# A transformer layer and a graph layer in one kernel: eight buffers for the projection's input, finer waits into the feed forward, graph tiles begun between the shared products

## The chip, the cores and the metric

One Trainium2 chip, one core of it. The metric is the device time of one execution in microseconds (us), as the median of several executions.

## The reference

`x` is 2 x 2048 x 512 in float32 (4096 rows), `cond` one vector of 512 per batch. Cut to what is computed:

```python
# layer 0: conditioned transformer block
h = ada_ln(x, cond, Wln1, bln1)                 # layer norm, scale and shift from cond @ W + b
x = x + attn(h, Wq, bq, Wk, bk, Wv, bv, Wo, bo) # 16 heads of 32, softmax over 2048 keys, @ Wo + bo
h = ada_ln(x, cond, Wln2, bln2)
x = x + gelu(h @ W1 + b1) @ W2 + b2             # 512 -> 2048 -> 512
# layer 1: graph attention over the first NG = 20 rows of each batch, two directions d
q_exp = where(x.sum(-1) == 0, 0, cond)
sf = concat([x, q_exp]) @ W_self.T + b_self
out = sf
for d in (0, 1):
    kv = sf[:, :20]                             # scores of each row against 20 rows, 16 heads
    aff = (sf @ Wq[d].T + bq[d]) . (kv @ Wk[d].T + bk[d]) / sqrt(32), masked by adj, + bias
    out = out + (softmax(aff) @ kv) @ Wout[d] + bout[d]
return x + relu(out)
```

## The kernel before, in words

The program is written out by hand: each engine has its own list of instructions in a fixed order, and engines meet only through semaphores. A function `pe_...`, `act_...`, `dve_...`, `pool_...` or `sp_...` issues work for TensorE, ScalarE, VectorE, GpSimd or SyncE (which issues nearly all DMAs and, as the others, waits in order). A semaphore's count is what is waited for: `s_om` counts projection tiles that TensorE has finished, and so on. Products of float32 matrices are made from a high part (rounded to the matmul's type) and a low part (what the rounding left): `TRI` lists the three pairs high*high, high*low, low*high, so a product over 512 takes 3 x 4 = 12 matmuls of 128x128 by 128x512.

The stages are: q, k, v with the first layer norm; attention (32 units `v` of four heads by 512 queries); the output projection; the feed forward (8 chunks of 512 rows, 16 blocks `q` each, 128 in all); the graph's shared products; the graph's 32 row tiles. The change touches three places.

**The output projection** (`sp_out`, `pe_out`, `act_out`, `dve_out`, `pool_out`, lines 1008 to 1101) runs over 32 tiles `t` of 128 rows. For one tile: SyncE loads the attention output from memory into `ao` (three buffers, L960) and the residual rows into `x2` (five buffers, L967, two tiles ahead, once the store of five tiles earlier has landed); ScalarE copies `ao` into the high part of `aT` (L1057, two buffers, two tiles ahead); VectorE subtracts for the low part (L1070); TensorE does the 12 matmuls (L1045) into one of three banks of PSUM; GpSimd adds the bias to the residual (L1101); VectorE adds PSUM and residual (L1077); SyncE stores it to `x2_d` (L1021). In VectorE's order tile t is added first and then tile t+2 is split. Beside this run, at fixed tiles, the last unit's reciprocals (tile 2), the load of the feed forward's first chunk `xinb` (1 MB, L1005, tile 6), its layer norm (VectorE at tiles 8 to 11, GpSimd at tile 10), its transposes (four on TensorE before tiles 16 to 19), and the splitting of eight blocks of feed-forward weights (tiles 20 to 27; five of them are loaded at tiles 20 to 24, each once VectorE has split an earlier one).

The first two tiles are split during the last attention unit, and `pe_out_tile(0)` stands before that unit's last two value products (L729).

**The way into the feed forward.** `out_over` (L1103) waits for everything of the projection, the landing of the last stores of `x2` with it. All five engines call it first in the feed forward; ScalarE then also waits for `b2B`, the second bias (`s_bias` at 96), which SyncE loads after its own `out_over` and after four weight blocks (L1471 to 1473). A block q of the feed forward is `pe_ff1(q)` (L1181, 12 matmuls into bank 4 or 5), gelu on ScalarE (L1292), its split on VectorE (L1303, L1305) and `pe_ff2(q)` (L1194, 12 matmuls into banks 0 to 3). TensorE's order is ff1(0), ff1(1), ff2(0), ff1(2), ff2(1), and so on. ScalarE splits two weight blocks after each of the first 12 gelus (L470).

**The graph's start.** `pe_graph_shared` (L1571) makes products that all tiles share: `pe_ww`, `pe_gg` (L1547, split into `gg` by ScalarE L1600 and VectorE L1626), `pe_vw(0)`, `pe_vw(1)` (L1558, 16 matmuls each, masked into `vw` by VectorE L1633), and `pe_rows(0..3)` (L1567, 4 small matmuls each). Each of the four results of `pe_rows` goes through one buffer `rt`: ScalarE L1267, then VectorE L1312, L1314, L1317, one after the other. Only then do the tiles begin: `turn_x(0)` (transposes L1709, split by ScalarE L1801 and VectorE L1849), ScalarE's row sum (`act_zero`, L1795), VectorE's test of it (`dve_zero`, L1844), its transpose on TensorE (`turn_nz`, L1716), VectorE's edge terms (L1858 to 1867), the same for tile 1, and then score(0) (L1728, 24 matmuls, and L1734).

## Time and profile before

| | us |
|---|---|
| median of 3 executions | 3128.03 |
| lowest, highest | 3121.56, 3131.3 |
| the profiled execution, whole | 3132.72 |
| its span, first to last instruction | 3131.3 |
| TensorE busy in the span | 3076.8 (98%) |
| VectorE busy | 2156.5 (69%) |
| GpSimd busy | 1542.9 (49%) |
| ScalarE busy | 1388.4 (44%) |

Times in the views count from the span's start. "PE" is TensorE's matmuls, "PEld" its weight loads, "DVE" VectorE, "ACT" ScalarE, "POOL" GpSimd, "SPq" the queue in which SyncE issues DMAs. In brackets behind a piece of the timeline stands how long the engine was idle before it, and who ended that. PEclk is the share of the full clock that TensorE was granted.

### The profile page before, as it was taken

What the parts mean: (1) busy time and instruction counts of PE and PEld (TensorE: products, weight loads), DVE (VectorE), ACT (ScalarE), POOL (GpSimd) and SP (SyncE); (2) the same over time, 40 slices, a digit from 0 to 9 for tenths busy, and PEclk for the clock granted to TensorE, in tenths of its full rate; (3) what the DMA queues carried; (4) which work ended last, traced back from release to release, by engine and by line L of the source; (5) the groups of instructions that cost most, each with busy time, mean ns of one, the idle gap of its engine ahead of it and who ended that gap; (6) DMA issues with size and microseconds to landing.
All of it is one profiled execution on the core that took longest, in us unless ns stands there. A gap on an engine that the chain in (4) does not pass through costs nothing.

```text
span 3131.3 us, 42990 instructions
## 1 busy us (share of the span) xinstructions
PE 3076.8 (98%) x16138; PEld 2144.6 (68%) x16138; DVE 2156.5 (69%) x3633; ACT 1388.4 (44%) x2703; POOL 1542.9 (49%) x655
## 2 busy tenths in 40 slices
PE   8999999999999999999999999899999999999999
PEld 7887655555555555555555546688888888778998
DVE  4457889998999999989999976443333333237776
ACT  2221466666666666666666672221111111013333
POOL 0000389889888898898898973200000000102222
PEclk9999999999999999999999999999999999899999
DMA  6674687879779788797887776520111110212221
GB/s 206 187 228 150 175 169 169 193 150 198 167 165 201 151 189 174 167 199 150 181 182 160 164 155 230 187 81 6 35 41 41 41 41 29 98 59 68 78 82 61
DMA packets 169366, 423.39 MB, mean 135 GB/s; under 512 B 18493, under 2 KB 60605, under 8 KB 141864
## 3 DMA queue, kind: packets, MB, share of 16 engines
q0 software_dynamic: 27744, 201.08, 31.7%
q1 hardware_dynamic: 139639, 214.07, 22.8%
q10 hardware_dynamic: 1776, 5.51, 0.7%
q8 instruction: 128, 2.10, 0.3%
q14 instruction: 79, 0.64, 0.1%
HBM read 143.51 MB, written 75.50 MB: 70 GB/s over the span
## 4 chain that ended last, share of the span: by engine, by line
PE 94%; DVE 2%; DMA 2%; issue 1%; POOL 1%; ACT 1%; SPq 0%; DVEq 0%; ACTq 0%; POOLq 0%
PE ps L384 16%; PE ps L672 15%; PE ps L683 15%; PE ps L1194 12%; PE ps L1181 11%; PE ps L460 5%; PE ps L1728 4%; PE ps L464 3%; PE ps L1745 3%; PE ps L689 2%; PE ps L1766 1%; PE ps L1045 1%; PE ps L1531 1%; PE ps L158 1%; PE ps L293 1%
## 5 line engine op out<-in xcount | busy, mean ns | idle before, releaser
L397 DVE TENSOR_REDUCE nmp<-ps 128x1 f32<-128x512 f32 x1966 | 1200.0, 681 | 108.2 <-PE ps L384 103.9
L762 ACT ACTIVATE pt<-ps 128x512 f32<-128x512 f32 x2048 | 1031.0, 625 | 458.7 <-PE ps L672 455.5
L861 POOL TENSOR_TENSOR pt<-pt 128x2048 f32<-128x2048 f32 x217 | 995.9, 4589 | 119.6 <-ACT pt L762 113.3
L672 PE MATMUL ps<-qs,ks 128*128 128x512 f32 x2048 | 810.6, 400 | 2.5 <-ACT pt L762 2.5
L384 PE MATMUL ps<-ks,qs 96*128 96x512 f32 x1966 | 803.5, 409 | 0.1
L384 PEld LDWEIGHTS ps<-ks,qs 96*128 96x128 f32 x1966 | 372.6, 190 | 265.3 <-DVE nmp L397 167.8
L683 PE MATMUL ps<-pt,vq 128*32 128x512 f32 x4096 | 493.6, 599 | 0.0
L672 PEld LDWEIGHTS ps<-qs,ks 128*128 128x128 f32 x2048 | 389.4, 191 | 96.2 <-ACT pt L762 19.5
L1181 PE MATMUL ps<-hpb,w 128*128 128x512 f32 x1536 | 382.6, 399 | 3.4 <-DMA x_d<-x 3.4
L1194 PE MATMUL ps<-w,gp 128*128 128x512 f32 x1536 | 380.5, 396 | 3.1 <-DVE gp L1305 3.1
L1303 DVE CAST gp<-g 128x512 fp32r<-128x512 f32 x128 | 61.7, 482 | 403.7 <-ACT g L1292 403.7
L1194 PEld LDWEIGHTS ps<-w,gp 128*128 128x128 f32 x1536 | 289.4, 188 | 72.4 <-DVE gp L1305 3.5
L1181 PEld LDWEIGHTS ps<-hpb,w 128*128 128x128 f32 x1536 | 289.9, 191 | 70.2 <-issue 5.6
L1292 ACT ACTIVATE g<-ps,b1c 128x512 f32<-128x512 f32 x128 | 88.2, 689 | 535.9 <-PE ps L1181 535.9
L1425 POOL TENSOR_TENSOR res<-res,b2B 128x512 f32<-128x512 f32 x32 | 41.7, 1332 | 493.7 <-DMA res<-x_d 493.7
L683 PEld LDWEIGHTS ps<-pt,vq 128*32 128x32 f32 x4096 | 106.9, 109 | 245.4 <-ACT pt L762 163.1
L139 POOL TENSOR_SCALAR ve<-mv 128x4 f32<-128x4 f32 x16 | 4.0, 250 | 383.5 <-DVE mv L134 383.5
L853 POOL DMA_DIRECT2D pt<-pt x189 | 166.3, 880 | 42.3 <-PE ps L683 36.7
L866 POOL TENSOR_TENSOR pt<-pt 128x2048 f32<-128x2048 f32 x31 | 142.6, 4600 | 7.5 <-DMA pt<-pt 2.9
L493 ACT ACTIVATE st<-ps,bqk 128x512 fp32r<-128x512 f32 x64 | 43.9, 689 | 227.7 <-PE ps L460 224.6
L1728 PE MATMUL ps<-gg,xp 128*128 128x320 f32 x768 | 121.7, 314 | 0.0
L790 DVE RECIPROCAL accs<-accs 128x128 f32<-128x128 f32 x128 | 115.9, 930 | 0.0
(169 smaller groups left out, 2874.9 us busy)
## 6 DMA issues: line engine op xcount, KB each, us to landing
pt<-pt POOLq DMA_DIRECT2D x189, 1024.0 KB, 8.7
qk_d<-st SPq DMA_DIRECT2D x128, 256.0 KB, 2.9
qs<-qk_d SPq DMA_DIRECT2D x87, 256.0 KB, 5.0
ks<-qk_d SPq DMA_DIRECT2D x42, 512.0 KB, 8.5
xina<-in_x SPq DMA_DIRECT2D x8, 1024.0 KB, 6.4
v_d<-vst SPq DMA_DIRECT2D x32, 256.0 KB, 3.1
vq<-v_d SPq DMA_DIRECT2D x32, 256.0 KB, 4.3
ao_d<-accs SPq DMA_DIRECT2D x32, 256.0 KB, 7.1
```

The costliest lines, as they stand in the source:

```text
L384: pe.matmul(ps[:, ring.bank["max", u], :], qsb[0:96, v % 3, hq // 4, 128 * (hq % 4):128 * (hq % 4) + 128], ksb[w % 2][0:96, hq // 4, CH * ...
L397: dve.tensor_reduce(nmp[:, n // 4, n % 4:n % 4 + 1], ps[:, ring.bank["max", u], :], AX.X, ALU.max, negate=True).then_inc(s_mr, 1)
L460: m = pe.matmul(ps[:, bank, :], w[:, x, k, col:col + 128], hp[:, y, k, :], start=(i == 0 and k == 0), stop=(i == 2 and k == NK - 1))
L672: pe.matmul(ps[:, score_bank(n), :], ksb[w % 2][:, hh, 128 * kt:128 * kt + 128], qsb[:, v % 3, hh, :], start=True, stop=True).then_inc(s_s ...
L683: m = pe.matmul(ps[32 * hh:32 * hh + 32, 7, :], vq[:, kt, 32 * hh:32 * hh + 32], pt[:, exp_slot(g), hh, :], start=(kt == 0), stop=(kt == 15))
L762: act.activation(pt[:, exp_slot(g), hh, :], ps[:, score_bank(n), :], ACT.Exp, scale=SCALE).then_inc(s_exp, 1)
L853: pool.dma_start(accumulator(v, 1 + d), pt[:, exp_slot(g), :, :], accum_op=ALU.add).then_inc(s_dma[d], 16)
L861: pool.tensor_tensor(accumulator(v, 0), accumulator(v, 0), pt[:, exp_slot(g), :, :], ALU.add).then_inc(s_add, 1)
L866: pool.tensor_tensor(accumulator(v, 0), accumulator(v, 0), accumulator(v, 2), ALU.add).then_inc(s_add, 1)
L1181: m = pe.matmul(ps[:, 4 + r, :], w1[:, f // 4, x, k, 128 * (f % 4):128 * (f % 4) + 128], hp[:, y, k, :], start=(i == 0 and k == 0), stop=( ...
L1194: m = pe.matmul(ps[:, t, :], gp[:, q % 2, x, 128 * t:128 * t + 128], w2[:, f // 4, y, f % 4, :], start=(i == 0 and f == 0), stop=(i == 2 a ...
L1728: pe.matmul(ps[:, 1 + d, 0:320], xp[:, j, x, 128 * k:128 * k + 128], gg[:, b, y, k, 320 * d:320 * d + 320], start=(i == 0 and k == 0), sto ...
```

## The change

The input of the projection gets eight buffers: three as before and five, `ao5`, that lie where the last unit's keys were, so that loads of tiles 3 to 7 wait for the last score product. They are issued together at the head of `sp_out`, and after that each load runs seven tiles ahead. `aT` has four buffers and is filled three tiles ahead; on VectorE the split of tile t+3 now stands before the add of tile t. TensorE goes into ff1(0) after waiting for `s_accs` alone and waits for `s_oo` (the projection's adds) before ff1(1); ScalarE goes into gelu(0) after `s_ol` and waits for `out_over` and `b2B` only before gelu(1), behind the first two weight blocks. In the graph's start the four `pe_rows` stand before `pe_vw(0)`, and tile 0's transposes between `pe_vw(0)` and `pe_vw(1)`, with the matching moves on ScalarE and VectorE. No instruction is added or removed.

```diff
-        aT = place("aT", [128, 2, 2, D], base + 16384, F32R)
+        aT = place("aT", [128, 4, 2, D], base + 16384, F32R)
+        ao5 = place("ao5", [128, 5, D], base + 32768)
...
+        s_a8 = s_a3 + s_vq + [s_kd[0]]
...
         def sp_load_ao(t):
-            if t >= 3:
-                sp.wait_ge(s_ol, t - 2)
+            if t >= 8:
+                sp.wait_ge(s_ol, t - 7)
...
         def sp_out():
+            sp.wait_ge(s_sc, 64 * NU)
+            for t in range(3, 8):
+                sp_load_ao(t)
             for t in range(NT):
                 if t + 2 < NT:
                     sp_load_residual(t + 2)
-                if t + 3 < NT:
-                    sp_load_ao(t + 3)
+                if t and t + 7 < NT:
+                    sp_load_ao(t + 7)
...
         def act_out_turn(t):
...
-            if t >= 2:
-                act.wait_ge(s_om, t - 1)
+            if t == 2:
+                act.wait_ge(s_sc, 64 * NU)
+            elif t >= 4:
+                act.wait_ge(s_om, t - 3)
...
         def act_out():
+            act_out_turn(2)
             for t in range(NT):
-                if t + 2 < NT:
-                    act_out_turn(t + 2)
+                if t + 3 < NT:
+                    act_out_turn(t + 3)
...
         def dve_out():
+            dve_out_turn(2)
             for t in range(NT):
+                if t + 3 < NT:
+                    dve_out_turn(t + 3)
                 dve.wait_ge(s_om, t + 1)
                 dve.wait_ge(s_ob, t + 1)
                 dve.tensor_tensor(x2[:, t % 5, :], ps[:, (1, 2, 0)[t % 3], :], x2[:, t % 5, :], ALU.add).then_inc(s_oo, 1)
                 if t == 0:
                     dve_sums(NU - 1)
-                if t + 2 < NT:
-                    dve_out_turn(t + 2)
...
         def pe_ff():
-            out_over(pe)
+            pe.wait_ge(s_accs, NU)
             pe_ff1(0)
             for q in range(NQ):
+                if q == 0:
+                    pe.wait_ge(s_oo, NT)
...
         def act_ff():
-            out_over(act)
-            act.wait_ge(s_bias, 96)
+            act.wait_ge(s_ol, NT)
+            act.wait_ge(s_bias, 80)
             for q in range(NQ + 1):
+                if q == 1:
+                    out_over(act)
+                    act.wait_ge(s_bias, 96)
...
-            for b in range(B):
-                pe_vw(b)
             for n in range(4):
                 pe_rows(n)
+            pe_vw(0)
+            pe_turn_x(0)
+            pe_turn_nz(0)
+            pe_vw(1)
...
             act.wait_ge(s_wvl, 1)
+            weights_read(act)
+            act_zero(0)
+            act_turn_x(0)
+            act_turn_nz(0)
...
+            for n in range(4):
+                dve_rows(2 + n, n % 2, (5, 6, 3, 4)[n], D + 320 * (n // 2), 320)
+            weights_read(dve)
+            dve_zero(0)
+            dve_edges(0)
+            dve_turn_x(0)
             for b in range(B):
                 dve.wait_ge(s_vwm, b + 1)
...
-            for n in range(4):
-                dve_rows(2 + n, n % 2, (5, 6, 3, 4)[n], D + 320 * (n // 2), 320)
...
         def pe_graph():
-            for t in range(2):
-                pe_turn_x(t)
-                pe_turn_nz(t)
+            pe_turn_x(1)
+            pe_turn_nz(1)
```

(ScalarE's and VectorE's lists of the tiles lose tile 0 in the same way. Where `ao` was indexed by t modulo 3, the new `ao_slot` picks by t modulo 8.)

VectorE's list where the projection begins, before. `L1070` splits a tile (`aT<-ao`), `L1077` adds it (`x2<-ps`), L785 and L790 belong to the last attention unit:

```order
L799 TENSOR_TENSOR pt_79<-pt_79 128x2048 [waits s_add,s_exp]
L1077 TENSOR_TENSOR x2_94<-ps,x2_94 128x512 [waits s_ob,s_om]
L785 COPY accs_81<-ps 128x512 [waits s_ao,s_end]
L1070 TENSOR_TENSOR aT_95<-ao_93,aT_95 128x512 [waits s_oh]
L1077 TENSOR_TENSOR x2_94<-ps,x2_94 128x512 [waits s_ob,s_om]
L1070 TENSOR_TENSOR aT_95<-ao_93,aT_95 128x512 [waits s_oh]
```

The same place now (`ao5_96` are the five new buffers, L1082 splits and L1092 adds):

```order
L799 TENSOR_TENSOR pt_79<-pt_79 128x2048 [waits s_add,s_exp]
L1082 TENSOR_TENSOR aT_95<-ao_93,aT_95 128x512 [waits s_oh]
L1082 TENSOR_TENSOR aT_95<-ao5_96,aT_95 128x512 [waits s_oh]
L1092 TENSOR_TENSOR x2_94<-ps,x2_94 128x512 [waits s_ob,s_om]
L785 COPY accs_81<-ps 128x512 [waits s_ao,s_end]
L1082 TENSOR_TENSOR aT_95<-ao5_96,aT_95 128x512 [waits s_oh]
```

Tiles 2 and 3 are split before tile 0 is added; from then on a split stands three tiles ahead of the add behind it.

ScalarE's list at the way into the feed forward, before (the table of gelu, gelu(0), two weight blocks, gelu(1)):

```order
L1292 ACT_TABLE_LOAD [waits s_x21,s_x22,s_x20,s_x23,s_lo,s_x24,s_bias,s_wlo,s_f1,s_oo]
L1292 ACTIVATE g32_98<-ps,b1c_90 128x512 [waits s_om]
L470 ACTIVATE w1_85<-wtf_101 128x512 [waits s_wt0]
L470 ACTIVATE w1_85<-wtf_101 128x512 [waits s_wt1]
L1292 ACTIVATE g32_98<-ps,b1c_90 128x512 [waits s_f1]
```

And now:

```order
L1310 ACT_TABLE_LOAD [waits s_f1,s_bias]
L1310 ACTIVATE g32_99<-ps,b1c_90 128x512 [waits s_ol]
L470 ACTIVATE w1_85<-wtf_102 128x512 [waits s_wt0]
L470 ACTIVATE w1_85<-wtf_102 128x512 [waits s_wt1]
L1310 ACTIVATE g32_99<-ps,b1c_90 128x512 [waits s_x21,s_x22,s_x20,s_x23,s_lo,s_x24,s_bias,s_wlo,s_f1,s_oo,s_om]
```

The long wait has moved from the table load to gelu(1); the table load still waits for ff1(0) (`s_f1`).

TensorE's list at the graph's start, before (`vw` is L1558, `rows` L1567, `turn_x` L1709, `turn_nz` L1716, score L1728):

```order
L1558 MATMUL ps<-woT_108,kvr 120x512 [waits s_qst7,s_cw_o1,s_prep,s_ggl]
L1558 MATMUL ps<-woT_108,kvr 120x512 x3
L1558 MATMUL ps<-wcT,kvr 120x512 x4
L1567 MATMUL ps<-khb,lqw 4x80 [waits s_ggl]
L1567 MATMUL ps<-khb,lqw 4x80 x3
L1709 MATMUL ps<-ident,xt 128x128 [waits s_ggl,s_x30]
L1709 MATMUL ps<-ident,xt 128x128 x3
L1716 MATMUL ps<-ident,nzt 4x128 [waits s_nzv]
L1709 MATMUL ps<-ident,xt 128x128 [waits s_xl,s_x31]
L1709 MATMUL ps<-ident,xt 128x128 x3
L1716 MATMUL ps<-ident,nzt 4x128 [waits s_zT,s_nzv]
L1728 MATMUL ps<-gg,xp 128x320 [waits s_vw,s_xl]
```

And now (`rows` L1585, `vw` L1576, `turn_x` L1737, `turn_nz` L1744, score L1756):

```order
L1585 MATMUL ps<-khb,lqw 4x80 [waits s_ggl]
L1585 MATMUL ps<-khb,lqw 4x80 x3
L1576 MATMUL ps<-woT_109,kvr 120x512 [waits s_qst7,s_cw_o1,s_prep,s_ggl]
L1576 MATMUL ps<-woT_109,kvr 120x512 x3
L1576 MATMUL ps<-wcT,kvr 120x512 x4
L1737 MATMUL ps<-ident,xt 128x128 [waits s_ggl,s_x30]
L1737 MATMUL ps<-ident,xt 128x128 x3
L1744 MATMUL ps<-ident,nzt 4x128 [waits s_nzv]
L1576 MATMUL ps<-woT_109,kvr 120x512 [waits s_qst7,s_cw_o1,s_prep,s_ggl]
L1737 MATMUL ps<-ident,xt 128x128 [waits s_xl,s_x31]
L1744 MATMUL ps<-ident,nzt 4x128 [waits s_zT,s_nzv]
L1756 MATMUL ps<-gg,xp 128x320 [waits s_vw,s_xl]
```

The second group of `vw` now stands behind tile 0's two transposes, the second of which waits for VectorE (`s_nzv`). On VectorE tile 1's test stands behind the masking of `vw(1)`.

## Rows read from the trace of the kernel before

**Rows 1.** The page: the chain that ended last, by engine.
```profile
PE 94%; DVE 2%; DMA 2%; issue 1%; POOL 1%; ACT 1%; SPq 0%; DVEq 0%; ACTq 0%; POOLq 0%
```

**Rows 2.** Instructions by line, 1889.2 to 1999.2 us: busy, mean ns | idle before.
```profile
L1045 PE MATMUL ps<-wo,aT 128*128 128x512 f32 x372 | 92.9, 409 | 13.0 <-DVE aT L1070 13.0
...
L1101 POOL TENSOR_TENSOR x<-x,boB 128x512 f32<-128x512 f32 x29 | 40.1, 1385 | 65.1 <-DMA x<-in_x 65.1
L1070 DVE TENSOR_TENSOR aT<-ao,aT 128x512 fp32r<-128x512 f32 x30 | 23.4, 780 | 17.2 <-ACT aT L1057 16.8
L1077 DVE TENSOR_TENSOR x<-ps,x 128x512 f32<-128x512 f32 x31 | 21.2, 685 | 22.6 <-PE ps L1045 19.7 <-POOL x L1101 2.9
L1057 ACT ACTIVATE aT<-ao 128x512 fp32r<-128x512 f32 x29 | 18.3, 632 | 78.8 <-DMA ao<-ao_d 39.4 <-PE ps L1045 39.4
```

**Rows 3.** Timeline of PE in the projection: start, us, what, xcount, idle before.
```profile
1889.12 11.46 PE L1045 MATMUL ps<-wo,aT 128*128 128x512 f32 x48
...
1927.22 13.01 PE L1045 MATMUL ps<-wo,aT 128*128 128x512 f32 x48 [2.98 <-DVE aT L1070]
1943.30 0.60 PE L158 MATMUL ps<-ident,xinb 128*128 128x128 f32 x4
...
1982.81 13.00 PE L1045 MATMUL ps<-wo,aT 128*128 128x512 f32 x48 [2.33 <-DVE aT L1070]
```

**Rows 4.** Windows: length, busy of the five engines, PEclk, DMA share, GB/s.
```profile
1902.00:1916.40 14.40, 14.26 (x60) 11.19 (x60) 6.62 (x10) 1.90 (x3) 5.12 (x5) 1.00 0.96 316
...
1927.20:1934.00 6.80, 6.78 (x23) 5.33 (x24) 6.06 (x8) 0.63 (x1) 3.55 (x3) 0.75 0.74 250
1934.00:1964.00 30.00, 30.00 (x139) 24.30 (x137) 22.72 (x29) 9.42 (x15) 12.25 (x9) 1.00 0.70 233
```

**Rows 5.** DMA issues 1875 to 2015 us: KB each, median us to landing.
```profile
x_d<-x SPq DMA_DIRECT2D x32, 256.0 KB, 2.5
...
x<-in_x SPq DMA_DIRECT2D x29, 256.0 KB, 3.6
...
xinb<-x_d SPq DMA_DIRECT2D x1, 1024.0 KB, 7.6
```

**Rows 6.** Chain that ended last, way into and in the feed forward: start, us, what.
```profile
1996.56 2.00 DMA x_d<-x
...
2000.63 5.50 DMA b2B<-in_b
...
2006.30 1.28 ACT L1292
...
2009.62 4.61 PE ps L1194 x12
...
2050.24 2.80 PE ps L1194 x12
```

**Rows 7.** Timeline of PE there.
```profile
1999.23 7.31 PE L1181 MATMUL ps<-hpb,w 128*128 128x512 f32 x24 [3.42 <-DMA x_d<-x]
```

**Rows 8.** Timeline at the graph's start, PE and VectorE.
```profile
2792.16 8.64 DVE L1626 TENSOR_TENSOR gg<-ps,gg 128x320 fp32r<-128x320 f32 x16 [0.52 <-ACT gg L1600]
...
2799.77 3.69 PE L1558 MATMUL ps<-woT,kvr 128*120 128x512 f32 x8
...
2813.70 2.38 PE L1567 MATMUL ps<-khb,lqw 128*4 128x80 f32 x32
2813.80 0.75 DVE L1633 TENSOR_TENSOR vw<-ps,bm 120x384 f32<-120x384 f32 x2 [6.12 <-PE ps L1558]
...
2821.87 0.54 DVE L1317 SCALAR_TENSOR_TENSOR rows<-rt,sel 4x320 fp32r<-4x320 f32 x1
...
2822.55 0.37 PE L1716 MATMUL ps<-ident,nzt 128*4 128x128 f32 x1 [5.89 <-DVE nzt L1844]
...
2826.16 5.27 PE L1728 MATMUL ps<-gg,xp 128*128 128x320 f32 x24
...
2834.54 3.68 PE L1728 MATMUL ps<-gg,xp 128*128 128x320 f32 x24
```

More of the change, by code:

```diff
@@ L932, in program @@
         cursor[0] = chain_end
-        ao = take("ao", [128, 3, D])
+        ao3 = take("ao", [128, 3, D])
         x2 = take("x2", [128, 5, D])
-        aT = place("aT", [128, 2, 2, D], base + 16384, F32R)
+        aT = place("aT", [128, 4, 2, D], base + 16384, F32R)
+        ao5 = place("ao5", [128, 5, D], base + 32768)
         assert cursor[0] <= top - 16384
@@ L953, in ff_part, with ao_slot @@
             return w2[:, c0, 0, k - 4, :], w2[:, c0, 1, k - 4, :]
+        def ao_slot(t):
+            return ao3[:, t % 8, :] if t % 8 < 3 else ao5[:, t % 8 - 3, :]
         def sp_load_ao(t):
[L956 to L957 removed]
+            if t >= 8:
+                sp.wait_ge(s_ol, t - 7)
             if t % 4 == 0:
                 sp.wait_ge(s_ao, 16 * (16 * (t // 16) + 13 + t % 16 // 4))
[L960 removed]
+            sp.dma_start(ao_slot(t), ao_d[t]).then_inc(s_a8[t % 8], 16)
         def sp_load_residual(t):
@@ L1664, in program @@
         s_xt, n_xt = s_x3, [(NT - 1 - i) // 5 + 1 for i in range(5)]
-        s_ad, n_ad = s_a3, [(NT - 1 - i) // 3 + 1 for i in range(3)]
+        s_ad, n_ad = s_a3, [(NT - 1 - i) // 8 + 1 for i in range(3)]
         s_st, n_st = s_x2, [(NT - 1 - i) // 5 + 1 for i in range(5)]
@@ L1818, in act_graph @@
         def act_graph():
-            weights_read(act)
-            for t in range(2):
-                act_zero(t)
-                act_turn_x(t)
-                act_turn_nz(t)
+            act_zero(1)
+            act_turn_x(1)
+            act_turn_nz(1)
             for t in range(-1, NT):
@@ L1905, in dve_graph @@
         def dve_graph():
-            weights_read(dve)
-            for t in range(2):
-                dve_zero(t)
-                dve_edges(t)
-                dve_turn_x(t)
+            dve_zero(1)
+            dve_edges(1)
+            dve_turn_x(1)
             for t in range(-1, NT):
```

10 lines of the change are left out of this document (5 added, 5 removed).

## The prediction, made before the changed kernel ran

> **What bounds the kernel now.** I read the page's chain of waits first: TensorE is 94% of it [rows 1], so time can be won only where TensorE stands idle or runs at a low clock. The windows by stage, read next, leave three such places, and the change touches all three: the projection, the way into the feed forward, the graph's start. From 2040 to 2756 us TensorE has no idle time, and from 2826 us on next to none.
>
> *The projection.* Tile 1 begins at 1889.12 and the last tile ends at 1982.81 + 13.00 = 1995.81 [rows 3]: 106.7 us for 31 tiles, 3.44 a tile. Twelve such matmuls in a row take 2.80 [rows 6]. The lines of this stretch say who is waited for: TensorE waits 13.0 us for VectorE's split, VectorE 16.8 for ScalarE's copy, ScalarE 39.4 for the load of `ao` [rows 2]. So the load is late, and with three buffers it can't be issued earlier. Idle time costs more than itself: 48 matmuls should take 4 x 2.80 = 11.2 us, but behind two of the idle pieces (2.98 and 2.33 us) they take 13.0 [rows 3]. The windows show why: behind the first the granted clock is 0.75, a mixture of the 1.2 and the 2.4 GHz level, and then 1.00 [rows 4].
>
> *The way in.* From the last tile's end at 1995.81 to the end of ff2(0) at 2009.62 + 4.61 = 2014.23 pass 18.4 us for three products of 2.80. In them: 3.42 idle for the landing of the last store, 24 matmuls in 7.31, idle time until gelu(0) is split, and ff2(0) in 4.61 [rows 6, 7].
>
> *The graph's start.* The products end, and then four small results go through ScalarE and VectorE before tile 0 is tested: from the first of `pe_rows` at 2813.70 to the last VectorE row at 2822.41. TensorE is idle for 5.89 us there, does 0.37, and reaches score(0) at 2826.16, which takes 5.27 where the next takes 3.68 [rows 8].
>
> **The change, part by part.**
>
> *Eight buffers, four `aT`, three tiles ahead.* Loads of tiles 3 to 7 start when the last score product is done, some 10 us before tile 1, and later ones seven tiles, about 20 us, before use; the largest landing in these rows, 7.6 us for 1 MB [rows 5], fits in that. So the wait for `ao` goes. If nothing else is late, 31 tiles take 31 x 2.80 = 86.8 us and four transposes at most 4 x 0.60 = 2.4 [rows 3]: 89.2 instead of 106.7, a gain of 17.5.
>
> What is late next? (a) The residual, which keeps its five buffers. Tile t+2's is issued right behind the store of tile t-1, so three tiles form a ring: add 0.69, store's issue 0.4, landing L, bias 1.39 on GpSimd [rows 2], 2.5 + L in all, against 3 x 2.80 = 8.4. At the median L of 3.6 [rows 5] that is 6.1, so it isn't the limit; it becomes one at L = 5.9. Besides, TensorE may run two tiles ahead of the adds in its three banks, so 5 us of lateness are absorbed. (b) The DMA engines. A tile moves three times 256 KB, 0.79 MB, in 2.8 us: 281 GB/s, where the busiest stretch moved 316 at a share of 0.96, hence a ceiling near 330 by my estimate [rows 4]. That is enough for a tile. Not enough is it at tiles 20 to 24, when each also loads a weight block (1.05 MB, 3.2 us at 330), 5 x 0.4 = 2 us late in all; nor right behind `xinb` and the store of `accs` at tiles 6 and 7, 1.3 MB or 4 us of extra queue, which the rest of 330 - 281 drains only slowly. L then rises to 7 or so for a few tiles. Both lots are within the 5 us, but not by much. (c) VectorE. The layer norm of the first chunk goes through it and GpSimd at tiles 8 to 11; now its waits come after the split of tile t+3, not before it, so aT is full while they last. I take 1.0 us for what leaks out of (a) to (c): gain **16.5**, between 17.5 and 10.
>
> For VectorE there is a price that I weigh apart. Its split takes 0.78 us in the mean [rows 2], though most take 0.69: pieces that run beside GpSimd's bias add are longer. The Trainium skill, "SBUF — State Buffer", section "SBUF: two separate sides", has a rule for it: a VectorE operation with two inputs in SBUF and a GpSimd operation that reads SBUF exclude each other for the whole instruction. By it alone a tile at 20 to 27 costs VectorE up to 3 x 0.69 + 1.39 = 3.5 us, more than TensorE's 2.80, 8 x 0.7 = 5.6 us over the eight tiles; less the 5 us that the banks absorb, the sum would be 0.6 us smaller. By the rows the mean cost is 0.09 a split, and VectorE is busy for 22.72 of 30.00 us where TensorE never stops [rows 4]; I go by the rows.
>
> *The first two tiles* and everything before 1889 us stay as they are: the two splits that now stand before tile 0's add take 1.4 us and lie beside 7 us of TensorE's own work. Cost 0.
>
> *Finer waits.* Let T be the end of the last tile. ff1(0) now starts at T, as `s_accs` was reached long ago; ff1(1) wants only the last add, T + 0.7. They end at T + 5.6. gelu(0) wants ff1(0): table load 1.28, then what the chain shows from 2007.58 to 2009.62 for gelu and split, 2.0 [rows 6], so ff2(0) can start at T + 2.9 + 3.3 = T + 6.2, 0.6 late, and ends at T + 9.0. ff2(1), due at T + 11.8, wants gelu(1), which now carries the long wait: `b2B` landed at 2006.13, T + 10.3, and SyncE's order ahead of it is unchanged. With gelu 0.7, split 1.2: T + 12.2, 0.4 late. Relative to T the end of ff2(0) was 18.4 and is now 9.0, with 0.4 lost behind it: gain **9.0**. The clock stays up if the pieces of idle time are this short. The weight blocks 8 and up keep their times relative to T while TensorE is 9 us earlier. Blocks 8 to 11 are wanted by ff1(4) at T + 21 and blocks 12 to 15 by ff2(4) at T + 29; two blocks are split after each gelu, 5.6 us apart, and each reload wants about 4 us: by my count block 15 is split at T + 27. That is 2 us of reserve; if landings here took 7 us, about 4 us would be lost. Ends: 10 and 4.
>
> *The graph's start.* `pe_rows` now waits for all of `gg`, ready at 2792.16 + 8.64 = 2800.80, where `vw` waited for all but two: 1.0 us idle. Rows 2.4, then 13.9 for both `vw` (2799.77 to 2813.70), and 0.6 and 0.4 for tile 0's transposes [rows 3, 8]: 2818.1. The chain of the rows takes 8.7 from their start, to 2809.6, and the test of tile 0 comes just behind it; TensorE asks for that at 2800.85 + 2.4 + 6.9 + 0.6 = 2810.8. One microsecond of cover: were the chain 3 us longer, 2 us would be lost. Behind `vw(1)` VectorE masks for 0.75 and only then tests tile 1, while TensorE transposes x for 0.6: with the 0.37 of `turn_nz(1)`, score(0) starts at 2818.1 + 1.25 = 2819.4 instead of 2826.16, 6.8 earlier, and takes 3.7 instead of 5.27 as TensorE has hardly been idle [rows 8], 1.6 more. Gain **8.4**, between 5 and 9.4. Tile 1's own split lies beside score(0) and self(0), as before.
>
> **Sum.** 16.5 + 9.0 + 8.4 = 33.9 us off the profiled execution, 3132.7 to 3098.8. That execution is 4.7 us above the median of the three shown; from the median, 3128.0, it is **3094**. A measurement of this kernel tells 0.3%, 9.4 us, from no change.
>
> **The rivals.**
>
> 1. *The residual ring takes over.* If L is 7.6, the largest in the rows, all through the stage, a tile takes (2.5 + 7.6) / 3 = 3.37 instead of 2.80, 17 us over 31 tiles: nearly all of the projection's gain is gone and the time is 3111. For it: the stage wants 281 GB/s of some 330, and landings rise when queues fill. Against: TensorE ran 30 us without a stop at 233 GB/s and a DMA share of 0.70 [rows 4], with the same ring. In half the stage: 3103. Chance of a loss of 6 us or more this way: 0.12.
> 2. *The feed forward starves for weights*, at TensorE's earlier pace: 5 us lost, 3099. Chance 0.10.
> 3. *The change doesn't do what it says at the graph's start*: TensorE asks for tile 0's test before it is there, and `vw(1)`, queued behind that wait, slips with it. 3 us lost, 3097; inside the forecast's range. Chance 0.06.
> 4. *Slower than before.* The same ring with landings so long that the stage is longer than today. It must lose the other gains, 17.4, and 9.4 besides: 106.7 + 26.8 = 133.5 us, 4.31 a tile, a ring of 12.9 us, L = 10.4. Then 3138. No landing in these rows is over 7.6. Chance 0.02.
>
> 5. *The DMA engines are full at tiles 20 to 24*, and the adds are already late by what the banks absorb: 5 tiles at 3.2 us instead of 2.80, 2 us lost, 3096. Chance 0.05. The Trainium skill, "DMA: Bandwidth & Descriptors", section "Specifications", puts the limit of a core's HBM traffic at about 358 GB/s; by that estimate the five tiles would take 2.93 us each and lose 0.7 us. No row of this trace holds such a rate for a whole tile.
>
> **How the numbers follow.** Forecast as summed, with small leaks: 0.65. Low ends together (10 + 4 + 5 = 19) give 3109, high ends (17.5 + 10 + 9.4 = 36.9) 3091, and the executions of before scatter by 6.5 below and 3.3 above their median. Range 3085 to 3109; rival 1 in full and rival 4 lie outside. Faster by over 0.3% wants more than 9.4 of 34 us: all cases but rival 4 and half of the worst of rival 1: 0.94. Within: 0.04. Slower: 0.02.
>
> **What would show it.** In the changed profile: ScalarE's wait for the DMA of `ao` in the projection near 0 instead of 39.4; TensorE's idle time there under 2 us and its clock 1.00 throughout; the stage about 90 us long; GpSimd's wait for the residual still the longest, but never passed on to TensorE. ff1(0) directly behind the last tile, then two idle pieces of about half a microsecond, no store and no `b2B` before ff1(0). TensorE idle for 1 us before the rows and under 1 us before score(0), and score(0) in 3.7. I am wrong if VectorE's add waits for GpSimd and TensorE for the add (`s_oo`), if ScalarE waits for weight blocks and TensorE stops in the feed forward's first 30 us, or if the total falls by less than 20 us.

## The result, and the profile after

| | before | after |
|---|---|---|
| median of the runs, us | 3127.06 (3121.56 to 3131.3, 4 runs) | 3095.74 (3094.47 to 3096.06, 4 runs) |
| ratio | | 0.9900, 95% interval 0.9883 to 0.9917 |
| profiled execution, us | 3132.7 | 3095.97 |
| its span, us | 3131.3 | 3094.5 |
| its mean granted clock | 0.990 | 0.995 |

Forecast was 3094, range 3085 to 3109: the kernel is faster by 31 us, and the time is 1.7 above the forecast. The spans differ by 36.8 us, more than the medians. Stage by stage, from the starts and ends on TensorE's timeline:

| stage | before | after | gain | forecast |
|---|---|---|---|---|
| start of the kernel to tile 1's start | 1889.12 | 1889.42 | -0.3 | 0 |
| projection: tile 1 to the last tile's end | 106.69 | 90.81 | 15.9 | 16.5 |
| way in: to ff2(1)'s start | 20.98 | 13.03 | 7.95 | 9.0 |
| ff2(1) to the first graph product (`pe_ww`) | 746.02 | 741.37 | 4.65 | none |
| graph products, up to score(0) | 63.35 | 55.91 | 7.44 | 6.8 |
| score(0)'s start to TensorE's last | 302.36 | 301.15 | 1.2 | 1.6 |

The last row holds score(0) itself, 5.27 before and 3.75 after. Five rows are near the forecast; one, 4.65 us, was not on the list.

**The projection.** First who waits for whom in that stage of the changed kernel (waiting line, what it waits for, us in total, times, longest):

```profile
ACT aT L1068 <- PE ps L1054: 48.0, 23, 4.3
POOL x L1114 <- DMA x<-in_x: 46.4, 23, 8.8
DVE x L1092 <- POOL x L1114: 11.4, 8, 2.6
...
PE ps L1054 <- DVE x L1092: 1.3, 2, 1.0
```

ScalarE's wait for the load of `ao`, 39.4 before [rows 2], is not there any more; ScalarE waits for TensorE alone, as the engine that runs ahead should. TensorE's 13.0 for the split have become 1.3, and for another thing: the add, `L1092`. Its timeline shows both pieces:

```profile
1889.42 33.87 PE L1054 MATMUL ps<-wo,aT 128*128 128x512 f32 x144
1924.30 3.04 PE L1054 MATMUL ps<-wo,aT 128*128 128x512 f32 x12 [1.01 <-DVE x L1092]
1927.64 6.04 PE L1054 MATMUL ps<-wo,aT 128*128 128x512 f32 x24 [0.31 <-DVE x L1092]
```

Twelve tiles without a stop, then 1.01 and 0.31 idle. Both are short, and the windows of the stage (length, busy time of the five engines, granted clock, DMA share, GB/s) show that the clock did not fall behind them, unlike [rows 4]:

```profile
1889.40:1924.30 34.90, 33.89 (x149) 27.01 (x145) 22.56 (x34) 7.59 (x12) 15.34 (x12) 1.00 0.85 286
1924.30:1930.60 6.30, 5.99 (x24) 4.32 (x24) 6.30 (x9) 0.63 (x1) 3.00 (x3) 1.00 0.74 234
1930.60:1980.20 49.60, 49.60 (x222) 40.14 (x222) 39.50 (x49) 16.19 (x26) 25.29 (x17) 1.00 0.81 278
```

The DMA engines carried 278 to 286 GB/s, about the 281 of the forecast, for nearly the whole stage, at median landings only a little longer than before [rows 5]: 3.5 to 4.4 us for 256 KB. But `xinb` took 8.8, and the longest landing of a residual 8.5.

```profile
x_d<-x SPq DMA_DIRECT2D x30, 256.0 KB, 3.5
x<-in_x SPq DMA_DIRECT2D x29, 256.0 KB, 4.0
...
wtb<-in_W SPq DMA_DIRECT2D x8, 256.0 KB, 4.4
xinb<-x_d SPq DMA_DIRECT2D x1, 1024.0 KB, 8.8
```

That one landing begins the chain to the idle piece of 1.01. SyncE issued it 1.7 us after the load of `xinb` (1905.93):

```profile
1907.60 8.53 DMA x<-in_x
...
1917.93 0.69 DVE x L1092
1918.62 1.20 DVE bst L130 x2
...
1921.04 1.04 POOL rstd L142
...
1923.46 0.69 DVE x L1092
```

The residual is late, so an add is late, so the layer norm's statistics (`bst`) behind that add, so GpSimd's part of the norm (`rstd`), so the next bias add behind `rstd`, and with it the add that TensorE waits for.

**The way in.** TensorE's timeline, to hold against [rows 6, 7]:

```profile
1980.07 5.63 PE L1194 MATMUL ps<-hpb,w 128*128 128x512 f32 x24
1986.40 3.06 PE L1207 MATMUL ps<-w,gp 128*128 128x512 f32 x12 [0.71 <-DVE gp L1323]
...
1993.26 3.07 PE L1207 MATMUL ps<-w,gp 128*128 128x512 f32 x12 [1.05 <-DVE gp L1323]
```

ff1(0) stands directly behind the last tile, and ff1(0) and ff1(1) take 5.63, not 7.31. The two idle pieces are where the text put them, 0.71 for 0.6 and 1.05 for 0.4. The chain of waits says what the second waits for:

```profile
1974.48 4.40 DMA x<-in_x
...
1978.94 2.58 POOL x L1114 x2
...
1981.62 0.70 DVE x L1092
1982.34 2.00 DMA x_d<-x
...
1986.41 4.74 DMA b2B<-in_b
...
1991.33 0.70 ACT g L1310
```

It begins at the *residual*: the last add comes at 1981.62, 1.4 us behind the last tile's end, because GpSimd's bias add is late, where the forecast had it at once, as it was before (VectorE's timeline: 1995.84, for an end at 1995.81). Then store, weight blocks, `b2B`, gelu(1).

**The graph's start.** The same for [rows 8]:

```profile
2772.68 2.38 PE L1585 MATMUL ps<-khb,lqw 128*4 128x80 f32 x32 [1.05 <-DVE gg L1650]
...
2780.86 0.54 DVE L1335 SCALAR_TENSOR_TENSOR rows<-rt,sel 4x320 fp32r<-4x320 f32 x1
2781.33 0.15 DVE L1869 TENSOR_SCALAR nzt<-tsum 128x2 f32<-128x2 f32 x1
...
2782.38 0.27 PE L1744 MATMUL ps<-ident,nzt 128*4 128x128 f32 x1
...
2790.44 0.27 PE L1744 MATMUL ps<-ident,nzt 128*4 128x128 f32 x1 [0.48 <-DVE nzt L1869]
2790.54 3.75 PE L1756 MATMUL ps<-gg,xp 128*128 128x320 f32 x24
```

1.05 idle before the rows, tile 0's test done at 2781.48 and asked for at 2782.38 (0.9 of cover), 0.48 idle before tile 1's, score(0) in 3.75: all as worked out. That score(0) starts 7.44 us earlier and not 6.8 lies mostly in tile 0's transposes, which take 0.54 us of TensorE's time (2781.95 to 2782.49) where the sum had 0.6 + 0.4.

### The profile page after: what moved, and what is told of

It reads as the page before. It is cut to its first block, busy times and chain, and to the rows that moved or that the text cites. A ratio compares the mean times of both kernels' runs of the same rounds, so it can differ in the third digit from the quotient of the medians.

```text
span 3094.5 us, 42984 instructions
## 1 busy us (share of the span) xinstructions
PE 3063.0 (99%) x16138; PEld 2134.4 (69%) x16138; DVE 2157.8 (70%) x3633; ACT 1389.2 (45%) x2703; POOL 1546.5 (50%) x655
## 4 chain that ended last, share of the span: by engine, by line
PE 94%; DVE 2%; DMA 2%; POOL 1%; issue 1%; ACT 0%; SPq 0%; DVEq 0%; ACTq 0%; POOLq 0%
PE ps L384 16%; PE ps L672 15%; PE ps L683 15%; PE ps L1207 11%; PE ps L1194 11%; PE ps L460 5%; PE ps L1756 4%; PE ps L464 3%; PE ps L1773 3%; PE ps L689 2%; PE ps L1794 1%; PE ps L1549 1%; PE ps L158 1%; DMA x<-in_x 1%; PE ps L293 1%
## 5 line engine op out<-in xcount | busy, mean ns | idle before, releaser
L853 POOL DMA_DIRECT2D pt<-pt x189 | 166.0, 878 | 41.8 <-PE ps L683 36.8
L1756 PE MATMUL ps<-gg,xp 128*128 128x320 f32 x768 | 120.2, 312 | 0.0
L790 DVE RECIPROCAL accs<-accs 128x128 f32<-128x128 f32 x128 | 115.5, 926 | 0.0
```

What stands on the lines that cost most here:

```text
L853: pool.dma_start(accumulator(v, 1 + d), pt[:, exp_slot(g), :, :], accum_op=ALU.add).then_inc(s_dma[d], 16)
L1756: pe.matmul(ps[:, 1 + d, 0:320], xp[:, j, x, 128 * k:128 * k + 128], gg[:, b, y, k, 320 * d:320 * d + 320], start=(i == 0 and k == 0), sto ...
```

## The experiments

Twelve runs, in three lots: ten new kernels, and before and after once more. Each lot ran on one chip beside runs of before. One profile of each gives its stages (us):

| kernel | projection | way in | ff2(1) to `pe_ww` | to score(0) | score(0) |
|---|---|---|---|---|---|
| before | 106.69 | 20.98 | 746.02 | 63.35 | 5.27 |
| before again | 107.96 | 20.06 | 744.49 | 65.05 | 5.44 |
| after | 90.81 | 13.03 | 741.37 | 55.91 | 3.75 |
| after again | 93.65 | 13.84 | 744.84 | 55.92 | 3.76 |
| projection alone | 89.21 | 19.50 | 742.90 | 63.36 | 5.53 |
| waits alone | 108.58 | 11.81 | 741.29 | 63.36 | 5.49 |
| graph alone | 107.40 | 18.45 | 746.00 | 55.91 | 3.76 |
| buffers only | 103.62 | 18.43 | 744.46 | 63.36 | 4.75 |
| order only | 107.79 | 24.02 | 744.46 | 63.37 | 4.75 |
| split behind the add | 93.31 | 18.46 | 742.91 | 63.37 | 5.54 |
| split first, two deep | 99.28 | 18.54 | 741.27 | 63.36 | 5.71 |
| residual one ahead | 103.50 | 15.46 | 744.58 | 57.60 | 3.75 |
| small spread | 90.73 | 14.04 | 738.06 | 55.91 | 3.75 |
| all four | 93.59 | 10.88 | 737.97 | 55.91 | 3.76 |

**Each part alone** (first lot; before there 3129.03, 3125.48 to 3132.44). The diff of the change, cut in three: the buffers with their order, the waits of `pe_ff` and `act_ff`, and the graph's part; and before itself once more.

> The kernel before, unchanged, for a second profile. In the first pair of profiles the feed forward (start of ff2(1) to the first matmul of the graph's pe_ww) took 746.0 us before and 741.4 after, 4.7 us that no term of the prediction holds; they lie where matmuls of 2 and 40 columns stand between the blocks of the last chunk (4.81, 7.03, 5.03 and 4.59 us against 3.63, 5.48, 4.52 and 3.01). Theory: the granted clock falls there at a point of time that the change doesn't set, so this second profile shows another length, anywhere from 741 to 747 us. Rival: it belongs to the code as written before, and the stretch is 746.0 us again within 0.3. Projection 106 to 108 us in both.

> Only the projection's part of the change (eight buffers, four aT, split before add, three tiles ahead). My theory, that the three parts don't touch each other: tile 1's start to the last tile's end 91 us instead of 106.7 (two short waits for the add of about 1.3 us in all), the way in unchanged at 21.0, the graph's start unchanged (score(0) 63.4 us behind the first pe_ww matmul). Total 3110 to 3114, 16 less than before, give or take the clock in the last chunk. Rival, that part of the projection's gain came with the finer waits: 95 us or more and 3117.

> Only the finer waits into the feed forward. Theory: last tile's end to the start of ff2(1) 13.0 us instead of 21.0, projection 107, and the feed forward behind it of a length that the clock decides: total 3118 to 3122. Rival: the 4.7 us of the feed forward come from weights that are split earlier: then this kernel alone has 741.4 there, e1 and e3 746.0, and it gains 12 to 13 us, 3114.

> Only the graph's start. Theory: first pe_ww matmul to score(0) 55.9 us instead of 63.4 and score(0) in 3.75 instead of 5.27, everything before as it was: 9 us less, 3117 to 3121. Rival: score(0) stays at 5.3, as the clock falls over the rows in any case: 7.5 us less.

Measured: before again 3130.56 (one run); the projection alone 3113.88, ratio 0.9951 (0.9936 to 0.9966); the waits alone 3120.09, 0.9972 (0.9962 to 0.9981); the graph alone 3118.74, 0.9961 (0.9947 to 0.9975). Each part has its full gain in its own stage. The three gains add up to 34.4 us, near the 31.3 of the whole, so the three don't hang on each other as far as the intervals tell (each gain is uncertain by 3 to 5 us). The other stages move by up to 2.5 us, where before and before again differ by 0.9 to 1.7. The projection alone takes 89.21 us with TensorE never idle: the 89.2 that the prediction gave for "nothing else is late", and less than the 91 that I expected. Of the waits alone, one number is better than in the full change, 11.81 against 13.03: there tiles still come at the old pace, the last add waits for TensorE and not for GpSimd, and no idle piece stands before ff2(1).

In these profiles the stretch from ff2(1) to `pe_ww`, which no part touches but for its first microseconds, takes anything from 741.3 to 746.0, and before itself gives 746.0 and 744.5. So the rival of the first expectation (746.0 again within 0.3) is out. More on that below.

**Which half of the projection's edit carries it** (second lot, before there 3131.17; third lot, 3129.07). Buffers only keeps two of `aT` and the old order, order only keeps three of `ao`:

```diff
 # buffers only, against the projection alone
-        aT = place("aT", [128, 4, 2, D], base + 16384, F32R)
+        aT = place("aT", [128, 2, 2, D], base + 16384, F32R)
...
-                if t + 3 < NT:
-                    act_out_turn(t + 3)
+                if t + 2 < NT:
+                    act_out_turn(t + 2)
 # order only, against the projection alone
-            if t >= 8:
-                sp.wait_ge(s_ol, t - 7)
+            if t >= 3:
+                sp.wait_ge(s_ol, t - 2)
...
-            sp.dma_start(ao_slot(t), ao_d[t]).then_inc(s_a8[t % 8], 16)
+            sp.dma_start(ao_slot(t), ao_d[t]).then_inc(s_a3[t % 3], 16)
```

> The kernel before with the eight buffers and loads seven tiles ahead, and nothing else: aT keeps two buffers, two tiles ahead, the split behind the add. Stage: tile 1's start to the last tile's end, 106.7 to 108.6 us in four profiles of it as before, 89.2 and 90.8 with the whole change. Theory A, the late load is what counts: ScalarE's wait for the load of ao is near 0 and the stage takes 93 to 96 us; what is left are the waits behind VectorE's reciprocals and the layer norm, some 3 to 5 us with the clock. Theory B, the shallow aT and the split behind the add count: stage 100 us or more.

> The other half: four aT, three tiles ahead, split before the add, but three buffers for the input; its load goes four tiles ahead, which the earlier split allows. Theory A, the late load counts: 98 us or more, and ScalarE still waits 20 us or more for the load. Theory B, depth and order count: below 94 us.

Measured: 3124.22 and 3133.06, one run each; projection 103.62 and 107.79, so Theory B holds for the first and Theory A for the second. Four profiles of the projection as before give 106.69 to 108.58, four with the whole edit (projection alone, small spread, after, after again) 89.21 to 93.65. Against these, buffers only gives 3 to 5 us, order only nothing that stands out, both together 13 to 19. The waits of buffers only, then of order only:

```profile
ACT aT L1066 <- PE ps L1054: 74.5, 29, 7.9
...
PE ps L1054 <- DVE aT L1079: 8.6, 7, 3.1
```

```profile
ACT aT L1063 <- DMA ao<-ao_d: 79.5, 27, 8.7
...
DVE aT L1077 <- ACT aT L1063: 44.0, 21, 5.5
...
PE ps L1049 <- DVE x L1087: 9.4, 7, 3.7
```

With the buffers alone the load isn't waited for any more, but TensorE still waits 8.6 us for the split. With the order alone the load is as late as ever, 79.5 us, and the split, now ahead of the add, holds the add too. So the load was one of two limits of nearly the same size, and behind it stood a second one that [rows 2] do not show by name: two buffers of `aT` let ScalarE and VectorE begin a tile only when TensorE has left the one before last.

What that second limit is, depth or place, the third lot takes apart: depth without place (`dve_out_turn(t + 3)` moved behind the add of tile t, four of `aT`), place without depth (the buffers only, with `dve_out_turn(t + 2)` moved ahead of the add).

```diff
 # split behind the add, against the projection alone
-                if t + 3 < NT:
-                    dve_out_turn(t + 3)
                 dve.wait_ge(s_om, t + 1)
...
                     dve_sums(NU - 1)
+                if t + 3 < NT:
+                    dve_out_turn(t + 3)
```

> The projection's part alone (eight buffers, four of aT, ScalarE and the split three tiles ahead), but VectorE adds tile t first and splits tile t + 3 behind it. Theory A (the four buffers of aT are the half that matters: a split three tiles ahead is early even behind the add): projection 89 to 92, as with the whole part (89.2). Theory B (the place ahead of the add matters too, since stats and tests hold the add and with it the split): 96 to 104, with waits of TensorE for VectorE's split as in the kernel with the buffers only (103.6).

> Eight buffers for ao, two of aT, the split of tile t + 2 ahead of the add of tile t. Theory A (depth decides): ScalarE's copy still has to wait for tile t's last matmul, the split comes 1.9 us behind it and the add 0.8 later, so the projection stays near the 103.6 of the buffers only, 100 to 106. Theory B (the place decides: the split is no longer held by a late add): 90 to 94.

Measured: 3111.47 and 3116.06, one run each; projection 93.31 and 99.28. Depth alone brings 10.3 of the 14.4 us between 103.62 and 89.21, place alone 4.3. Neither theory holds cleanly, but depth is the larger half (93.31 is just above the 92 of Theory A). What place is worth is not shown. At depth four, 93.31 lies within the 89.21 to 93.65 of the four profiles with the whole edit; at depth two, 103.62 and 99.28 are one profile each and differ by no more than those four do. What happens without the place is on TensorE's timeline of the kernel that splits behind the add:

```profile
1922.44 3.07 PE L1054 MATMUL ps<-wo,aT 128*128 128x512 f32 x12 [2.27 <-DVE aT L1082]
1926.51 5.86 PE L1054 MATMUL ps<-wo,aT 128*128 128x512 f32 x24 [0.99 <-DVE aT L1082]
```

These are the tiles of the layer norm: VectorE waits 2.88 us for a bias add that GpSimd holds, and the split stands behind it. With the split ahead, after again stops at the same tiles for 2.46 us, now for the add.

**The residual's ring.** The changed kernel with the residual one tile ahead, not two, which makes the ring two tiles long. It is rival 1 made true:

```diff
-                if t + 2 < NT:
-                    sp_load_residual(t + 2)
+                if t and t + 1 < NT:
+                    sp_load_residual(t + 1)
```

> The changed kernel with the residual loaded one tile ahead instead of two. By my ring (add 0.7, store's issue 0.4, landing L, bias 1.4, so 2.5 + L over now two tiles) and the median landing of 3.6 a tile takes 3.05 us instead of 2.80, and the stage 31 x 3.05 + 2 = 97 us instead of 90.8; at L = 4.4, 107 us. Rival, the ring is no limit because TensorE's three banks hide it: 91 to 93 us.

Measured: 3113.12 (one run), projection 103.50. The waits:

```profile
POOL x L1114 <- DMA x<-in_x: 69.1, 26, 19.8
...
DVE x L1092 <- POOL x L1114: 39.7, 19, 6.8
...
PE ps L1054 <- DVE x L1092: 9.1, 7, 4.0
```

This is the chain DMA, GpSimd, VectorE, TensorE that the prediction named as the sign of rival 1, so the ring exists. Its sum does not give its size: the residual's landings had a median of 3.5 us, for which the expectation has 97 us or less, and the stage took 103.50. TensorE ran the first ten tiles without a stop; then it waited 3.98 us at the norm and six times more, up to 1.91 us at tiles 25 to 28, and its matmuls ran slower behind the longest piece (48 in 14.43 us, for 11.5). So the median landing does not set it; that single late landings do is likely (the longest was 8.1 us), but not shown. With two ahead, TensorE waits for the add only at the norm and, in after again, once more for 0.38 us.

**The stretch nobody forecast.** From ff2(1) to the 32 matmuls of 2 columns (`L1225` before, `L1238` after) pass 667.1 to 667.3 us before, after, and in every experiment that leaves these matmuls in place, but for one that comes below. Behind that point they part. Before and after, on TensorE's timeline:

```profile
2683.95 4.81 PE L1225 MATMUL ps<-condT,wcT 128*128 128x2 f32 x32
2688.61 7.03 PE L1232 MATMUL ps<-xT,wvT 128*128 128x40 f32 x32
2695.44 5.03 PE L1181 MATMUL ps<-hpb,w 128*128 128x512 f32 x12
```

```profile
2660.50 3.63 PE L1238 MATMUL ps<-condT,wcT 128*128 128x2 f32 x32
2663.99 5.48 PE L1245 MATMUL ps<-xT,wvT 128*128 128x40 f32 x32
2669.27 4.52 PE L1194 MATMUL ps<-hpb,w 128*128 128x512 f32 x12
```

The same instructions, 16.9 and 13.6 us. TensorE is busy all the time, and still the granted clock falls: 0.82 from 2662 to 2700 us before; 0.91 after. The moment of the fall differs: it meets the first group before, only the second one after. From the first group to `pe_ww` the kernels that keep these matmuls together take 74.1 to 78.9 us. The rival of the waits' experiment, that weights split earlier make the stretch short, is out: the split first, two deep has before's waits and 741.27, the change once more has the new ones and 744.84. What sets the moment of the fall is open. The small spread moves the groups apart, eight small matmuls between every three large ones:

```diff
+                if ci == LAST and f == 6:
+                    pe_qt(t)
+                if ci == LAST and f == 7:
+                    pe_kv(t)
...
-                for n in range(NK):
-                    for k in range(NK):
-                        m = pe.matmul(ps[:, 7, 2 * n:2 * n + 2], wcT[:, k, 128 * n:128 * n + 128], condT2[:, k, :],
```

> The changed kernel with the 32 small matmuls of 2 columns and the 32 of 40 columns in the last chunk no longer in one piece behind ff2(6), but four groups each between the groups of ff2(6) and ff2(7). From ff2(1) to the 2-column matmuls 667.2 us passed in all six profiles; from there to pe_ww 74.1 to 78.9. Theory, that this spread is the clock falling over a piece in which TensorE streams few columns: now nothing falls there, the feed forward takes 738 to 739.5 us instead of 741.4, and the total is 2 to 4 us below the changed kernel's 3095.7, with less scatter than the kernel before has. Rival: small matmuls cost the same wherever they stand, 741.4 again.

Measured: 3090.49 (3088.87 to 3093.92, 4 runs), ratio to before 0.9870 (0.9853 to 0.9886). The window of 38 us over the same work (columns as above):

```profile
2662.00:2700.00 38.00, 38.00 (x185) 26.36 (x185) 9.47 (x19) 3.24 (x5) 2.36 (x7) 1.00 0.25 83
```

Clock 1.00, and the stretch takes 738.06, as the theory has it; the rival is out. So the fall costs 3 us where it comes late (741.4) and 8 where it comes early (746.0). The total is 5.2 under the changed kernel's 3095.7, on another chip, for 2 to 4 expected; the smaller scatter that was expected does not show, the four runs span 5 us.

**All together, and the change once more** (third lot). The four edits: the residual three ahead, `b2B` loaded at tile 28 with the weight blocks ahead of the wait for the last store, Gelu's table loaded before the wait for the last split, the small spread.

```diff
-                if t + 2 < NT:
-                    sp_load_residual(t + 2)
+                if t + 3 < NT:
+                    sp_load_residual(t + 3)
...
+                if t == 28:
+                    sp.wait_ge(s_ol, 27)
+                    sp.dma_start(b2B[:, :], row("b2")).then_inc(s_bias, 16)
...
-            act.wait_ge(s_ol, NT)
             act.wait_ge(s_bias, 80)
+            act.activation(warm[:, :], b1c[:, 0:1], ACT.Gelu)
+            act.wait_ge(s_ol, NT)
...
-            out_over(sp)
+            sp.wait_ge(s_om, NT)
             for n in range(8, 12):
                 sp_ff_weights(n)
-            sp.dma_start(b2B[:, :], row("b2")).then_inc(s_bias, 16)
+            out_over(sp)
```

> The changed kernel with four more edits: residual loads three tiles ahead, b2's row loaded at tile 28 with the last feed forward weights no longer behind the last store, Gelu's table called before the wait for the last split, and the small matmuls of the graph's first products spread over the last chunk (as in the small spread). Theory A (each of the late things named is what its stage waits for): projection 89.5 to 90.3 (the two idle pieces of 1.01 and 0.31 gone), way in 12.0 to 12.7 (the 0.71 before the third shared product of ff2(0) stays, the 1.05 before ff2(1) goes), ff2(1) to the first graph product 738.1 as in the small spread; time 3.5 to 6 us under the changed kernel on the same chip. Theory B (the way in is not set by the gelu behind b2, only by the work): way in 13.0 to 14.0 as before and only the spread's 3 to 4 us gained.

> The changed kernel once more, for the same chip. Theory A (the 4.65 us that the feed forward lost between the two profiles is a matter of when the clock falls, not of the change): ff2(1) to the first graph product anywhere from 741 to 746; projection 90 to 92, way in 12.8 to 14.1, graph start 55.9, all as in the first profile. Theory B (the change itself shortened it): 741.4 within 0.3 again.

Measured on one chip: all four 3091.3 (3091.0 to 3092.91), ratio to before 0.9878 (0.9864 to 0.9893); after again 3099.28 (3097.34 to 3102.38), 0.9901 (0.9884 to 0.9917). So the change's ratio comes back to a ten-thousandth, and the four edits take another 8.0 us off it; this is the fastest version beside the small spread, whose ratio is the same within the intervals. That the other three edits gain anything in the whole time is thus not shown. Between the two profiles (spans 3089.6 and 3100.9) lie 3.0 us in the way in, 1.9 in the products just behind it, 5.0 at the small matmuls, 1.2 behind score(0) and nothing in the projection.

After again answers the question of the 4.65 us. The same kernel has 744.84 in that stretch, not 741.37. Of the 3.5 us more, 1.6 lie behind the first small group, where its 32 matmuls of 40 columns take 7.03, as before's did. The other 1.9 lie ahead of it: `b2B` takes 5.37 us to land, an idle piece of 1.88 stands before ff2(1), and ff2(1) itself runs at the low clock, so that the small matmuls come after 669.09 us:

```profile
1996.13 4.60 PE L1207 MATMUL ps<-w,gp 128*128 128x512 f32 x12 [1.88 <-DVE gp L1323]
...
2668.76 7.03 PE L1245 MATMUL ps<-xT,wvT 128*128 128x40 f32 x32
```

Theory A holds for the stretch: its length is no property of the change. The projection (93.65 for 90 to 92) is outside what it expected.

In the way in, the four edits end the idle time altogether: no piece stands between the last tile and the products. The way in takes 10.88, below the 12.0 to 12.7 of Theory A: I had expected the 0.71 before ff2(0) to stay. Of the four edits only the table load of 1.28 us stands on gelu(0)'s path; none was run by itself.

```profile
1981.88 5.61 PE L1199 MATMUL ps<-hpb,w 128*128 128x512 f32 x24
1987.33 3.00 PE L1233 MATMUL ps<-w,gp 128*128 128x512 f32 x12
```

The projection is a miss: 93.59, not 90, with the residual a tile earlier. Its one idle piece, 2.45 us, is behind the norm. GpSimd's timeline of that kernel, then VectorE's:

```profile
1920.98 0.57 POOL L139 TENSOR_SCALAR ve<-mv 128x4 f32<-128x4 f32 x1 [8.26 <-DVE mv L134]
1921.70 1.04 POOL L142 TENSOR_TENSOR rstd<-ve,mhalf 128x4 f32<-128x4 f32 x1
1922.73 5.34 POOL L1119 TENSOR_TENSOR x<-x,boB 128x512 f32<-128x512 f32 x4
```

```profile
1916.80 1.29 DVE L130 BATCH_NORM_STATS2 bst<-xinb 128x6 f32<-128x512 f32 x2 [4.96 <-DMA xinb<-x_d]
...
1924.08 0.69 DVE L1097 TENSOR_TENSOR x<-ps,x 128x512 f32<-128x512 f32 x1 [2.62 <-POOL x L1119]
```

GpSimd stands 8.26 us in its fixed order before the norm's `ve`, with residuals landed behind it (it then does four bias adds without a wait). `ve` waits for VectorE's statistics, these for the landing of `xinb`. Here the edit itself made that late: its load landed in 8.7 us, as in after, but was issued 19.6 us behind tile 1's start, where the other four profiles have 16.5 to 16.7, since SyncE now issues before it a residual that waits for the store of one tile later. So what leaks in the projection is the 1 MB of `xinb`, by its own landing or by that of the residual queued behind it, through the order on GpSimd. Over the profiles with the changed order, the start of `rstd`, counted from tile 1's, and TensorE's idle time go together: projection alone 30.0 us and 0, small spread 31.4 and 1.1, after 31.6 and 1.3, all four 33.3 and 2.5, after again 33.2 and 2.8. This is a reading over five profiles; a kernel with the norm's two operations on another engine, or placed behind the next bias add, wasn't tried.

## Why the prediction was right, and where it wasn't

*The projection, 16.5: right, for 15.9 and, in the second profile of the change, 13.0 (106.69 less 93.65).* The base of 89.2 came out in the projection alone. The leak was put at 1.0 and is 1.6 and 4.4, the second still in the term's bounds. Its three sources were weighed one by one, and two of them act together. (a) hardly counts: the residual's median landing stayed at 4.0, under the 5.9 from which the ring decides. (b) was half right: the tiles with weight blocks ran without a stop, but behind `xinb` landings rose as the text said (8.5 us for a residual, for "7 or so"). (c), the norm, passes that on by a step that the text didn't have: not VectorE's time, but GpSimd's fixed order, where bias adds stand behind `rstd`. So the cover of 5 us, held against (b) alone, was not enough. That `aT` would be full there was right; it was the add that was missing.

*Why the load was late: only half the story.* The text followed TensorE to VectorE to ScalarE to the load, and gave the whole 17.5 to that. Buffers only shows 3 to 5 us for it. [Rows 2] had the rest in plain view: ScalarE's idle time was 39.4 for the load and 39.4 for TensorE. The change takes the load's wait away and lets ScalarE wait for TensorE two tiles further ahead (48.0 us of waiting are left, and cost nothing). The sum came out because the change deals with both; that the text, which priced one, was right about the 17.5 is in this respect luck.

*The port that VectorE and GpSimd share.* VectorE's split takes 0.68 alone; beside the bias add it is stretched to as much as 1.79, and its mean rose from 0.78 [rows 2] to 0.95. The add, which reads one input from PSUM, takes 0.68 to 0.69 in all cases, and the norm's statistics too. The prediction went by the mean of before, which was too small, but the 0.17 more a split (28 splits, some 5 us in the stage) lay in VectorE's spare time, save at the norm. By the Trainium skill ("SBUF — State Buffer", section "SBUF: two separate sides") a VectorE operation in a two-port mode, or with two SBUF inputs against a GpSimd operation that reads SBUF, excludes the GpSimd operation, and whichever starts first holds the other up for the whole instruction; the prediction told only the half on two inputs. The trace agrees on that half, and GpSimd's bias add is stretched too, from 1.29 to as much as 1.84. Stretched are also a cast (0.41 to 1.48) and the norm's scaling (0.53 to 1.51), with one input in SBUF; whether these run in the two-port mode no run here shows. The worst case, a split whole behind a bias add, would be 0.68 + 1.29 = 1.97; the longest took 1.79, and most tiles paid nothing, where the estimate let each of eight pay.

*The way in, 9.0 for 7.95.* Order and pieces were right. Mis-sized was the last add, taken as 0.7 behind the last tile and in truth 1.4 + 0.7 = 2.1, since the bias add is late: the store lands 4.1 us after the tile's end, where before it was 2.8. `b2B` took 4.74 for the 5.50 of [rows 6], which gave half of it back.

*The graph's start, 8.4 for 7.44 + 1.52 = 8.96,* less 0.3 later on. Its steps are within 0.2, but for tile 0's transposes, 0.54 for 1.0.

*Not in the sum: 4.65 us.* The prediction looked for time where TensorE stands idle or runs at a low clock, and passed over 2040 to 2756 us because TensorE has no idle time there. It had a clock of 0.82 in one window, and the page's row of the granted clock had an 8 in that place. The medians moved by 31.3, near the 33.9 of the sum, and the spans by 36.8. The 4.65 are part of the spans; how much of the difference is due to them no run shows, for the profiled execution of before was itself 5.7 above the median of its runs.

*The rivals.* 1: the ring is real (103.50 when shortened), but with two ahead it took no more than the leak above. 2: no wait of TensorE for weights in any profile; the 2 us of reserve held. 3: 0.9 of cover was enough. 4: far off. 5: over the last 50 us of the stage, tiles 20 to 24 among them, the DMA engines gave 278 GB/s and TensorE didn't stop.

## What to carry to other kernels

When the engine ahead of the bound one waits for two things in equal parts, one edit may be worth little: here 3 to 5 us and none alone, 13 to 19 together. Read the releasers' shares before you price an edit at the whole wait. A small operation that one engine must do for another, in a fixed order, is worth as much as what is queued behind it, and a buffer's cover is spent once: don't set it against each source of lateness by itself. One profile of a stage is one draw: the same projection took 89.2 to 93.7 us in four of them. And a stage without idle time can still lose to the clock, here up to 8 of 746 us: look at the granted clock, not only at who waits.

## What the runs showed of the hardware

- **The granted clock falls while TensorE is busy without a gap**: in all twelve profiles that keep them together it fell during 32 matmuls of 2 columns and 32 of 40 in a row, 9 to 12 us. The next twelve matmuls of 512 columns then take 4.2 to 5.5 us, where 2.9 is usual on these timelines. The same kernel takes 5.48 or 7.03 for the 40-column group in two executions. With eight small ones and three large ones in turn the clock stayed at 1.00 in both kernels that have them so, and the whole stretch took 738.06 and 737.97. Profiles with the same instructions in the stretch differ by up to 4.8 us, those of one kernel by 1.5 and 3.5; how much of the 10 us by which before's own runs differ comes from it, no run shows.
- **Short idle pieces leave the clock alone, long ones don't, and between them it goes either way.** On TensorE's timelines from 1884 to 2020 us of all fourteen profiles, ahead of matmuls of 512 columns, none of 51 idle pieces of 0.2 to 1.6 us was followed by more than 0.3 us of loss. Of 28 pieces of 1.75 to 3.1 us 18 were, and the matmuls behind them took 1.3 to 2.7 us longer: 4.60 for twelve behind 1.88, where 3.07 is usual behind a short piece, and 10.58 for 36 behind 2.45, where 8.68 is. Behind 2.27 twelve took 3.07, and the clock there was 1.00. All 12 pieces of 3.4 us and more cost 1.2 to 3.0 us.
- 256 KB landings stayed at 3.5 to 4.4 us in the median at 278 GB/s over the 91 us of the stage; single residuals queued behind the 1 MB load took up to 8.5, and 10.1 in after again.
